# A two-layer macaron block on one core: maxima of the second query chunk by differences of keys, first loads, and the scan for the largest weights

## The reference

```python
def _L0_ffn_ref(x, W_gate, W_qkv):                 # H = 16 heads of hd = 16
    gating = softmax(x @ W_gate.T)
    idx = argmax(gating); indicator = one_hot(idx, H)
    q, k, v = split(x @ W_qkv.T, 3)
    k_shared = einsum("bth,bthd->btd", indicator, k)          # each token: the key of its best head
    v_shared = einsum("bth,bthd->btd", indicator * max(gating), v)
    att = einsum("bhqd,bkd->bhqk", q, k_shared) / sqrt(hd)    # 16 heads of queries, one shared key
    y = einsum("bhqk,bkd->bhqd", softmax(causal(att)), v_shared)
    return y
...
x = x + 0.5 * _L0_ffn_ref(_layernorm(x), W_gate, W_qkv)       # layer 0
x = x + _L0_attn_ref(_layernorm(x), ...)                      # gates, h = (1-a)h + a*b, two products
x = x + 0.5 * _L0_ffn_ref(_layernorm(x), W_gate, W_qkv)       # layer 1
```

## Time and profile before

| | us |
|---|---|
| median of three executions (lowest, highest) | 901.45 (896.96, 907.77) |
| the profiled execution, its own time | 904.45 |
| its span, first to last instruction | 902.7 |
| outside of the span | 1.75 |
| mean granted TensorE clock | 0.963 |

### The profile page before, as it was taken

How to read it: one execution, slowest core, us unless ns; L and a number is a source line. 1 busy time by engine, 2 the same in 40 slices (tenths; PEclk the granted TensorE clock), 3 DMA queues, 4 the chain that set the end, 5 groups by cost and what they waited for, 6 DMA issues and landing times.

```text
span 902.7 us, 18417 instructions
## 1 busy us (share of the span) xinstructions
PE 844.9 (94%) x6300; PEld 282.7 (31%) x6300; DVE 778.2 (86%) x2252; ACT 691.8 (77%) x1142; POOL 298.0 (33%) x566
## 2 busy tenths in 40 slices
PE   8889779989999999999999899999999999999997
PEld 6433222333222233222432233333332323222221
DVE  5888998889998988979878998899989999999920
ACT  1127556566998989968878877888779998999996
POOL 4117314443111432325642445643431125110110
PEclk9889788989999999999999999999999999999999
DMA  6110000101000000010010001000010000000000
GB/s 185 49 42 20 1 1 1 60 1 60 2 2 1 1 2 1 2 59 2 1 59 2 2 1 42 20 1 25 1 60 2 2 26 2 24 1 2 1 2 23
DMA packets 20235, 17.97 MB, mean 20 GB/s; under 512 B 4128, under 2 KB 20144, under 8 KB 20144
## 3 DMA queue, kind: packets, MB, share of 16 engines
q1 hardware_dynamic: 19328, 16.00, 5.8%
q10 hardware_dynamic: 816, 0.80, 0.3%
HBM read 10.24 MB, written 6.29 MB: 18 GB/s over the span
## 4 chain that ended last, share of the span: by engine, by line
PE 50%; DVE 24%; ACT 10%; issue 10%; POOL 3%; DMA 1%; SPq 0%; POOLq 0%; DVEq 0%; ACTq 0%
PE ps L1752 16%; PE ps L1718 10%; DVE ps L1442 9%; PE ps L1740 9%; DVE mxp L1439 8%; ACT probs L1217 7%; PE ps L1636 3%; ACT relu L1205 2%; DVE mxp L1442 2%; PE ps L1641 2%; PE ps L1684 2%; PE ps L1651 1%; PE ps L1691 1%; POOL u L926 1%; DVE stats L1261 1%
## 5 line engine op out<-in xcount | busy, mean ns | idle before, releaser
L1217 ACT ACTIVATE probs<-ps 128x1024 f32<-128x1024 f32 (+5 forms) x843 | 556.2, 736 | 103.1 <-PE ps L1740 99.1
L1439 DVE TENSOR_REDUCE mxp<-ps 128x1 f32<-128x512 f32 x512 | 320.4, 682 | 20.7 <-PE ps L1718 16.6
L1752 PE MATMUL ps<-probs,v_l 128*32 128x512 f32 (+3 forms) x2560 | 304.6, 552 | 3.4 <-POOL probs L960 0.8
L1740 PE MATMUL ps<-q_t,k_tl 50*128 50x512 f16 (+3 forms) x1280 | 244.5, 357 | 21.0 <-DMA q_t<-m_row 9.2
L1718 PE MATMUL ps<-k_tl,q_t 48*128 48x512 f16 (+3 forms) x1152 | 249.4, 354 | 10.9 <-DVE mxp L1442 3.9
L1442 DVE CUSTOM_DVE_ANT_0 ps<-ps,mask 128x384 f32<-128x384 f32 (+3 forms) x512 | 233.6, 524 | 11.7 <-PE ps L1718 9.9
L960 POOL TENSOR_SCALAR_AFFINE_SELECT probs<-probs 128x256 f32<-128x256 f32 x256 | 103.2, 417 | 337.5 <-ACT probs L1217 336.1
L1718 PEld LDWEIGHTS ps<-k_tl,q_t 48*128 48x128 f16 x1152 | 73.9, 95 | 181.3 <-DVE mxp L1439 60.9
L1740 PEld LDWEIGHTS ps<-q_t,k_tl 50*128 50x128 f16 x1280 | 65.2, 94 | 188.2 <-ACT probs L1217 84.3
L1442 DVE CUSTOM_DVE_ANT_0 ps<-ps,relu 128x512 f32<-128x512 f32 x128 | 85.6, 716 | 8.2 <-PE ps L1718 7.3
L1442 DVE DVE_READ_ACCUMULATOR2_ANT mxp<- 128x1 f32 x640 | 89.2, 139 | 0.0
(11 more groups left out here) (181 smaller groups left out, 603.6 us busy)
## 6 DMA issues: line engine op xcount, KB each, us to landing
q_t<-q_scratch SPq DMA_DIRECT2D x96, 64.0 KB, 2.1
q_scratch<-q_part SPq DMA_DIRECT2D x16, 256.0 KB, 2.1
x_sb<-in_L_attn_x_dram SPq DMA_DIRECT2D x4, 512.0 KB, 8.2
out_dram<-x_sb SPq DMA_DIRECT2D x4, 512.0 KB, 3.0
q_t<-m_row SPq DMA_DIRECT2D x64, 4.0 KB
wqkv_n<-in_L_ffn_W_qkv_dram ACTq DMA_DIRECT2D x1, 768.0 KB, 6.9
w_in_sb<-in_L_attn_W_in_dram SPq DMA_DIRECT2D x1, 384.0 KB, 6.0
w_skip_sb<-in_L_attn_W_skip_dram SPq DMA_DIRECT2D x1, 256.0 KB, 5.5
```

The lines of the kernel that those rows point to most:

```text
L1217: last = a_.activation(out if len(banks) == 1 else out[:, n:n + 1, :], bank[:, :, P * i:QW], ACT.Exp, scale=SCALE / LIFT ** 2)
L1439: last = v_.tensor_reduce(to, scores, axis=AX, op=ALU.max)
L1740: last = mm(ps[:, BANK[e][n], P * i:QW], k_cols(ROWS_XM, hh, l, kt, P), q_rows(ROWS_XM, c, g, hh, P * i, QW - P * i), start=True, stop=True)
L1752: last = mm(out_bank[VW * hh:VW * hh + VW, P * i:QW], v_l[:, l, kt, :], probs[:, s % NB, hh, P * i:QW], start=j == 0, stop=j == key_tiles( ...
```

## The change

For units of chunk 1, the 16 part banks go. In their place the first 256 keys of chunk 0 are handled with the last 256: eight diff banks (two heads of 256 columns each, Relu by ACT) and eight over banks (two pieces of 256 columns each by DVE). The keys' differences (`kh_tl`) are made in `prepare(l, 0)`, with a `dpack` and a `dkeys` of two tiles. In `prepare(0, 0)` these two events stand ahead of the first maxima. The first load of x is cut in two, one on SP and one on ACT ahead of W_qkv; SP's other loads wait until W_qkv and W_gate have landed. `size` reduces absolute values at once instead of squaring into a buffer; `scale` needs no root from POOL. `WARM_UP`, the release steps in `SIDE_WORK` and several of the planner's prices change, so the order of all engines is made anew.

```diff
-WARM_UP = 5
+WARM_UP = 4
...
+HALF_TILES = (0, 1, 2, 3)
...
     for i in range(TC):
+        if c == 1 and i in HALF_TILES:
+            ahead.append((len(banks), i, None))
+            pair("over", 1, lambda par: [(h0 + par, i, QW // 2, QW // 2, h0 // 2 * (QW // 2)) for h0 in (0, 2)])
+            continue
...
-        banks[at - 4:at - 4] = [("diff", 1, [(h0 + par, i, 0, QW, 0)]) for par in range(2)]
+        banks[at - 4:at - 4] = [
+            ("diff", 1, [(h0 + par, i, 0, QW, 0)] if h0 is not None
+             else [(h + par, i, 0, QW // 2, h // 2 * (QW // 2)) for h in (0, 2)]) for par in range(2)]
...
-            ("kpack", l, c), ("keys", l, c)] + ([("dpack", l), ("dkeys", l)] if c == 1 else [])
+            ("kpack", l, c), ("keys", l, c)] + ([("dpack", l, c), ("dkeys", l, c)] if c < 2 else [])
...
-SIDE_WORK = [(-10, 5, prepare(0, 1)), (5, 5, [("bias",)]), (16, 23, [("size",)] + SPLIT), (28, 38, prepare(0, 2)),
-             (38, 38, prepare(0, 3)), (80, 101, branch(0)), (109, 123, prepare(1, 0)), (124, 130, branch(1)),
-             (134, 134, prepare(1, 1)), (153, 166, branch(2)), (166, 177, prepare(1, 2)), (180, 199, branch(3)),
-             (202, 212, prepare(1, 3))]
+SIDE_WORK = [(-7, 8, prepare(0, 1)), (18, 19, [("bias",)]), (19, 20, [("size",)] + SPLIT), (23, 28, prepare(0, 2)),
+             (38, 49, prepare(0, 3)), (79, 99, branch(0)), (102, 123, prepare(1, 0)), (123, 126, branch(1)),
+             (138, 148, prepare(1, 1)), (151, 160, branch(2)), (164, 169, prepare(1, 2)), (169, 192, branch(3)),
+             (221, 221, prepare(1, 3))]
...
-FIRST_X, FIRST_W = 6500.0, 8900.0
+FIRST_X, FIRST_W = 5500.0, 7600.0
...
-SAME_MODE, MAXIMA_FIRST, LOOK = 400, 500, 400
-AHEAD, LOSS = 12, (("PE", 0.75), ("DVE", 1.0), ("ACT", 1.0))
+SAME_MODE, MAXIMA_FIRST, LOOK = 400, 500, 300
+AHEAD, LOSS = 12, (("PE", 1.0), ("DVE", 1.0), ("ACT", 1.0))
...
-            sp.dma_start(bands(0), x[0, 0:QW, :].rearrange("(t p) d -> p t d", p=P)).then_inc(s_xld[0], 16)
+            sp.dma_start(bands(0)[:, 0:2, :], x[0, 0:2 * P, :].rearrange("(t p) d -> p t d", p=P)).then_inc(s_xld[0], 16)
+
+            sp.wait_ge(s_wqkv, 32)
...
+                    g_.tensor_tensor(k_diff[:, 0:2, :], k_in[:, 0:2, :], k_in[:, 2:4, :], op=ALU.subtract)\
+                        .then_inc(s_kd, 1)
...
-            def scale_root():
-                own(g_.memset(z_exp[:, :], -0.5))
-                pool.wait_ge(s_rd, FREED["scale", 1])
-                g_.tensor_tensor(z_root[:, :], z_sq[:, :], z_exp[:, :], op=ALU.pow).then_inc(s_zroot, 1)
...
+            act.dma_start(bands(0)[:, 2:4, :], x[0, 2 * P:4 * P, :].rearrange("(t p) d -> p t d", p=P))\
+                .then_inc(s_xld[0], 16)
...
-                    last = v_.tensor_tensor(to if n < DC else to.rearrange("p (a w) -> p a w", a=a), of, of, op=ALU.mult)
+                    last = v_.tensor_reduce(z_all[:, n:n + 1], of, axis=AX if n < DC else mybir.AxisListType.XY, op=ALU.max,
+                                            apply_absolute_value=True)
...
-                v_.tensor_reduce(z_part[:, 0:1], squared[:, 0:first], axis=AX, op=ALU.max)
-                v_.tensor_reduce(z_part[:, 1:2], squared[:, first:at], axis=AX, op=ALU.max).then_inc(s_size, 1)
+                v_.tensor_reduce(z_part[:, 0:1], z_all[:, 0:DC + 1], axis=AX, op=ALU.max)
+                v_.tensor_reduce(z_part[:, 1:2], z_all[:, DC + 1:DC + 3], axis=AX, op=ALU.max).then_inc(s_size, 1)
...
-                    v_.tensor_copy(z_sq[:, :], bank[:, 0:2]).then_inc(s_rd, 1)
-                    dve.wait_ge(s_zroot, 1)
-                    own(v_.tensor_scalar(z_mul[:, :], z_root[:, :], W_SIZE, None, ALU.mult))
-                    own(v_.reciprocal(z_rec[:, :], z_mul[:, :]))
+                    own(v_.tensor_scalar(z_rec[:, :], bank[:, 0:2], 1.0 / W_SIZE, None, ALU.mult))
+                    v_.reciprocal(z_mul[:, :], z_rec[:, :]).then_inc(s_rd, 1)
+                    dve.wait_ge(s_rd, FREED[e])
```

More of the change, by code:

```diff
@@ L171 @@
     "oev": (0, [("ACT", 480)]), "fin": (460, [("DVE", 700), ("POOL", 750)]), "out": (0, []),
-    "size": (0, [("DVE", 6400)]), "halve": (0, [("POOL", 1700)]),
+    "size": (0, [("DVE", 3600)]), "halve": (0, [("POOL", 1700)]),
     "join": (0, [("DVE", 750)]), "row": (100, [("ACT", 230)]),
@@ L202, in weights @@
     if e[0] == "scale":
-        return 100, "full", [("DVE", 3000 if e[1] else 900)]
+        return 100, "full", [("DVE", 2000 if e[1] else 900)]
     if e[0] == "split":
@@ L237, in needs @@
     if k in ("dpack", "dkeys"):
-        return [("keys", e[1], 1) if k == "dpack" else ("dpack", e[1])]
+        return [("keys",) + e[1:] if k == "dpack" else ("dpack",) + e[1:]]
     if k in ("bsum", "dev"):
@@ L352, in ready @@
             if kind_of(e) == "diff":
-                if ("dkeys", l) not in ended:
+                if ("dkeys", l, min(c, 2) - 1) not in ended:
                     return None
-                t = max(t, ended["dkeys", l] + TO_PE)
+                t = max(t, ended["dkeys", l, min(c, 2) - 1] + TO_PE)
             return max(t, ended["join", e[1]] + TO_PE) if e[0] == "row" else t
@@ L661, in macaron_block @@
         w_mul = sb("w_mul", [P, 2])
+        z_all = sb("z_all", [P, DC + 3])
         z_part = sb("z_part", [P, 2])
@@ L666, in macaron_block @@
         z_diag = sb("z_diag", [2, 2])
-        z_sq = sb("z_sq", [P, 2])
-        z_root = sb("z_root", [P, 2])
-        z_exp = sb("z_exp", [P, 2])
         z_mul = sb("z_mul", [P, 2])
@@ L721, in macaron_block @@
         kd_tl = sb("kd_tl", [P, 2, QW], f16)
+        kh_tl = sb("kh_tl", [P, 2, QW // 2], f16)
         probs = sb("probs", [P, NB, GH, QW])
@@ L780, in macaron_block @@
         s_size = sem("s_size")
-        s_zroot = sem("s_zroot")
         s_zmul = sem("s_zmul")
@@ L1016, in differences_rest @@
             def differences_rest(e):
-                pool.wait_ge(s_dk1, e[1] + 1)
-                parts = k_rows[:, :, :].rearrange("p t (g d) -> p t g d", d=HD)
-                g_.tensor_tensor(parts[:, :, 1::4, :], k_diff[:, :, :].unsqueeze(2).to_broadcast([P, TC, 2, HD]),
+                pool.wait_ge(s_dk1, NO[e] + 1)
+                n = 4 if e[2] else 2
+                parts = k_rows[:, 0:n, :].rearrange("p t (g d) -> p t g d", d=HD)
+                g_.tensor_tensor(parts[:, :, 1::4, :], k_diff[:, 0:n, :].unsqueeze(2).to_broadcast([P, n, 2, HD]),
                                  parts[:, :, 0::4, :], op=ALU.subtract).then_inc(s_drow, 1)
@@ L1091, in _ @@
                     halve(e)
-                elif e == ("scale", 1):
-                    scale_root()
                 elif e[0] in ("bias", "scan", "add", "bsum", "dev") or (e[0] == "gates" and e[2] == 0):
@@ L1119, in evict @@
                 elif e[0] == "dkeys":
-                    a_.activation(kd_tl[:, e[1], :], bank[:, 0:QW // 2].bitcast(f16), ACT.Copy).then_inc(s_ra, 1)
+                    to = (kd_tl if e[2] else kh_tl)[:, e[1], :]
+                    n = to.shape[1]
+                    a_.activation(to, bank[:, 0:n // 2].bitcast(f16), ACT.Copy).then_inc(s_ra, 1)
                 elif e[0] == "row":
@@ L1158, in differences @@
             def differences(e):
-                act.wait_ge(s_kd, e[1] + 1)
+                act.wait_ge(s_kd, NO[e] + 1)
+                n = 4 if e[2] else 2
                 act.wait_ge(s_fill, filled(TURNED[e]))
-                parts = k_rows[:, :, :].rearrange("p t (g d) -> p t g d", d=HD)
-                a_.activation(parts[:, :, 0::2, :], k_diff[:, :, :].unsqueeze(2).to_broadcast([P, TC, 4, HD]),
+                parts = k_rows[:, 0:n, :].rearrange("p t (g d) -> p t g d", d=HD)
+                a_.activation(parts[:, :, 0::2, :], k_diff[:, 0:n, :].unsqueeze(2).to_broadcast([P, n, 4, HD]),
                               ACT.Copy).then_inc(s_dk1, 1)
@@ L1254, in stats_of @@
                 if l == 0:
-                    dve.wait_ge(s_xld[c], 16)
+                    dve.wait_ge(s_xld[c], 16 if c else 32)
                 elif l == 1:
@@ L1440, in maxima @@
                         else:
-                            added = relu[:, PAIRED[e] % RELU_BUFS, :] if kind == "over" else mask[:, QW - w:QW]
+                            added = relu[:, PAIRED[e] % RELU_BUFS, col:col + w] if kind == "over" else mask[:, QW - w:QW]
                             last = v_.tensor_tensor_reduce(scores, scores, added, 1.0, LOWEST, ALU.add, ALU.max,
@@ L1661, in preparation @@
                     else:
-                        pe.wait_ge(s_drow, l + 1)
+                        pe.wait_ge(s_drow, NO[e] + 1)
                     keys = bank[:, 0:QW // 2].bitcast(f16)
-                    for t in range(TC):
+                    for t in range(2 if kind == "dkeys" and c == 0 else TC):
                         last = tr(keys[:, t * P:(t + 1) * P], k_rows[:, t, :], ident_h[:, :])
@@ L1713, in maxima @@
                     pe.wait_ge(s_ra, FREED["keys", l, c])
-                    if c > 1:
```

(5 more changed lines are left out.)

6 lines of the change are left out of this document (removed).

## The result

| | before | changed |
|---|---|---|
| median of four executions (lowest, highest), us | 904.61 (896.96, 908.39) | 890.95 (890.66, 891.59) |
| the profiled execution, its own time | 904.45 | 891.59 |
| its span | 902.7 | 889.9 |
| mean granted TensorE clock | 0.963 | 0.974 |

The ratio is 0.9856, with a 95% interval from 0.9806 to 0.9905: 13.7 us by the medians, 12.8 by the profiled spans. The four times of the changed kernel lie within 1 us of each other, those of the kernel before within 11: in 19 executions made with the experiments its median is 902.65, and the five above 907 us have a mean granted clock of 0.958 to 0.960, the others 0.962 to 0.969. Against 902.65 the gain is 11.7 us. The forecast was 888. The time is close to it; two of its terms were far off, one each way, as the experiments show.

A forecast was written before the change was run, and what follows sets the result against it. DVE was taken to bound layer 0's chunk-1 stretch, with three engines close together in layer 1's. Terms -15 - 1 - 1.1 + 1.0 = -16 from 904.45 gave 888 us, range 880 to 896 (873 to 903 with rivals).

The forecast's parts named there:

- Half keys in layer 0: Layer 0's chunk-1 stretch, 76 to 185 us: less DVE work, `size` included, shortens it by 15 us.
- Half keys in layer 1: Layer 1's chunk-1 stretch, 476 to 575 us: DVE's work moves to a nearly full ACT, gaining only 1 us.
- The new order: Whole kernel: side work moves a few steps within DVE's stretches; taken as 0, with 6 us to either side.
- A microsecond off DVE is worth nearly one: Layer 0, 76 to 185 us: DVE is busy 88% and ACT starved, so DVE savings shorten the stretch almost fully.
- Rival C: Layer 1's chunk-1 stretch: ACT becomes the pace and layer 0 returns only -5, giving 911 us; chance 0.11.
- Rival B: Chunk-1 stretches of both layers shrink with DVE, -18 in layer 0 and -9 in layer 1, giving 877 us; chance 0.17.
- `size`: Layer 0's DVE-bound stretch: DVE work falls by 3.1 to 3.3 us and a 0.92 us wait for POOL goes.
- The start: Up to the first products: x lands 1.1 to 1.4 us sooner with the new loads, for -1.1 us.
- The wait for `dkeys`: `prepare(0, 0)`, before the first maxima: PE waits for `dpack`, costing 1.0 us, bounds 0.3 to 1.5.
- Relu's cover: Four banks between a diff and its over bank hide the Relu; without them each pair would cost 0.6 us.
- PE's 1 us per layer: PE's 128 more multiplications over both layers, mostly overlapping, taken as 1 us per layer.

The follow-up runs named there:

- e5: The changed kernel, its order and banks kept, with chunk-1 units of both layers back at part banks and no Relu; 917.80 us.
- e7: The kernel before, its order and banks kept, with chunk-1 units made from half keys and chunk 0's `dpack` and `dkeys` behind `keys`; 925.54 us.
- e11: The changed kernel's order, but `dpack` and `dkeys` of the first chunk moved behind the eighth bank of unit 0; 896.05 us.

## Why the prediction came out right in sum and not in its terms

That the forecast is 3 us from the measured time is luck in good part: two errors, of about 12 and 16 us, cancel. In the order of its steps:

- **Half keys in layer 0: -15 with `size`.** Held. The part banks put back there cost 14.1, `size` 1.4, together 15.5. The trace shows a stretch of 94.3 (92 to 96 named), a clock of 0.87 (above 0.86 named), DVE at 82% (83% assumed). ACT is at 77%, not above 80%.
- **Half keys in layer 1: -1.** Mis-sized: -11.7 to -12.8. The failed step is "the relief goes to an engine that has no room to be relieved into". ACT's 77% belonged to the old order's stretch of 98.5 us. In the new order that stretch holds more side work (119.5 us with part banks) and ACT is busy 64% of it. The signs named there failed with it: 108.1 us instead of 97, ACT 84% instead of 93; DVE's 73% is near the 75 named.
- **The new order: 0, with 6 to either side.** Mis-sized: about +16.5. The kernel with part banks in the new order, `e5`, is 15.1 above the kernel before, though it has the new loads (-1.2) and `size` (-1.4); less 1.2 for the wait below, the order alone costs the old work about 16.5, an estimate from these four differences. The failed step is "side work moves by a few steps both ways, within stretches that are DVE's in either case". A spread of 10.8 us between executions of one kernel says nothing of what another order costs; a single planner number moved 8 to 10 us.
- **These two can't be parted from the half keys at all.** By the table, the half keys are worth -26.9 or +22.9, and the order +15 or -35, each according to the other. The sum "order 0, layer 0 -15, layer 1 -1" lands near the measured gain because layer 1 is wrong by -11.8 and the order by +16.5; the rest of the terms is within half a microsecond. The forecast gain of 16 is itself 2 to 4 us too large: 11.7 was measured against the 19 executions of the kernel before (902.65), 13.7 against the four of the first comparison.
- **"A microsecond off DVE is worth nearly one" in 76 to 185.** True in the new order (12.6 us for 12.8, with a clock of 0.87 instead of 0.82), false in the old one, where the busy shares had been read: there 13.0 us less of DVE made the stretch 10.7 longer. An engine at 88% of a stretch doesn't show that less of its work shortens the stretch. Rival C named such a loss, for ACT in layer 1; in the old order it came in both layers (layer 1's stretch in `e7`: 106.4 for 98.5), through late scores. Rival B's gain in layer 1 (-9) is near what the half keys bring there in the new order.
- **`size`: -3.1 to -3.3.** The work was right (3.6 us now, from 6.9), its worth 2.2 in the stretch and 1.4 by the end.
- **The start: -1.1.** Held: 1.2 by the medians, with ranges that touch, with x in use at 4.75 us (about 5 named). The Trainium skill (DMA: Bandwidth & Descriptors, "Issuing engines are not separate DMA queues") would have left x at 6.17 if the split alone counted. The runs don't contradict that rule, since the hold, which was to clear the way for W_qkv and x, was taken back with the split.
- **The wait for `dkeys`: +1.0.** Near at its place: 0.67 in `e11`; unit 0 joins 1.2 later in `e7` than before (44.2 against 43.0). No run shows what it costs by the end.
- **Relu's cover and PE's 1 us per layer.** No idle time before a relu piece is ACT's, and the new multiplications take 286 ns as in the earlier trace rows; nothing of their price was seen.

Not settled: which of the new parameters carries the gain that the order brings to the half keys, and what a fresh search of the parameters would give for either work. Of the 9.4 us by which the unchanged banks after layer 0's chunk 1 run shorter, 6.6 come with the order and not with the half keys, since with part banks in the same order (`e5`, 179.8 to 464.4) that stretch is 284.6.

## What to carry to other kernels

Where all engines follow one order written ahead, an edit has no price of its own: give the new work its order before judging it, and hold the order still to find what the work is worth. A busy share of 88% doesn't tell whether the engine holds the time. Look at whom PE waits for: where moving work from DVE to ACT paid, it had waited 35 to 37 us for DVE and 12 for ACT; where it cost time, 20.4 and 25.0 in layer 0, 14.8 and 13.9 in layer 1. These are four stretches of one kernel, not a rule. The sizes of work can be read from a trace to a few per cent (30.9 us forecast, 31.1 seen on DVE); the price of a new order can't, and deserves the widest term of the range.

## What the runs showed of the chip

A gap in PE's work at the start goes with a longer time at the lower clock. In `e11` PE stands still from 33.4 to 38.6 us; the granted clock is 1.00 in 32 to 35 us, 0.72 in 35 to 38 and 0.50 (1.2 GHz) from 38 to 53. In the changed kernel, whose longest gaps there are 1.78 and 0.50 us, it is 1.00 in 35 to 38, about 0.5 from 38 to 47 and 0.79 in 47 to 50. The end is 5 us later by the medians (896.05 against 890.95). The Trainium skill (TensorE: Matmul & The Clock Gate, "HAM oscillation — how this bites in real kernels") describes how waits between runs of multiplications return TensorE to its lower clock time after time; here the trace agrees in direction. One execution of four came at 890.82, with the highest mean clock of the four (0.980), so the same order can end with or without the loss; it left no trace that would show where they part.
